# Spreading x in f32, and joining the norm stage to the scan

## The chip, the cores and the metric

One core of a Trainium2 chip runs one program. Its five engines have a queue each: TensorE (PE, with its weight loads shown as PEld), VectorE (DVE), ScalarE (ACT), GpSimd (POOL) and SyncE (SP), which issues the DMAs. The metric is the device time of one execution in microseconds.

## The reference, cut to what matters

```python
x = sequence                                  # (1, 4096, 256)
x = x + ssm(layernorm(x))                     # the part that is changed
x = x + ffn(layernorm(x))
x = x + attention(layernorm(x))               # 16 heads of 16, 4096 x 4096 scores
x = x + ffn(layernorm(x))

def ssm(s):                                   # D = 256 channels, N = 16 states
    Bm, Cm = s @ W_B.T + b_B, s @ W_C.T + b_C
    Delta = softplus(s @ W_Delta.T + b_Delta + bias_Delta)     # one per position
    A_bar = exp(A * Delta)                                     # per channel and state
    B_bar = 1 / A * (A_bar - 1) * Bm
    state[t] = state[t-1] * A_bar[t] + s[t] * B_bar[t]
    y[t] = sum over the 16 states of state[t] * Cm[t]
```

All of it is f32. The four sums over positions and heads of the attention are the bulk of the kernel's time and are not touched by the change.

## The kernel before, in words

**Norm stage** (`norm_and_project`, up to line 412). The 4096 positions are taken in 8 chunks of 512. For a chunk, DVE takes statistics and normalises (L224, L228, L240), PE transposes the chunk (`turn`, L393), ACT copies the transposed f32 chunk out of PSUM (`copy_turned`, L330), and PE projects it (`project` in the new code, L408) to B, C and Delta, which are replicated so that each of the 128 partitions holds the value of its state; ACT adds the biases (`outputs`, L344). For the scan, the f32 values are also split into three bf16 parts, whose sum is the f32 value: ACT rounds (L334), POOL subtracts (L212), ACT rounds the rest (L338), DVE subtracts again (L247). DVE and ACT compute softplus by quarters of 1024 positions: -|z| (`minus_abs`, L254), exp (L350), log (L354), and the sum (L259). The FFN weights' angles are prepared beside this (L278 to L289). The stage is a block of its own: all engines meet at its end before the next block's first instruction.

**Scan stage** (`scan_to_projection`). A tile is 8 channels x 16 states on 128 partitions, by 1024 positions; 32 tiles cover the channels and 4 quarters the positions, so 128 tiles, n = 0 to 127, in that order. For a tile:
- PE spreads 8 channels of x over 128 partitions (`spread_x`, L717): a product with a 0/1 matrix, 2 halves of 512 positions, each the sum of three bf16 products. Its result goes to the PSUM pair `xr`, in the first tiles also to `yb`; `xr` is single, so the spread of tile m waits until DVE has read that of tile m-1 (`w_done`).
- DVE multiplies it by B (`times_b`, L969) into one of six buffers `w`.
- ACT computes the decay exp(A Delta) into PSUM (L871), and for the tiles of POOL a second time into SBUF, minus one (`decay_less_one`, L857, L860). Its carry out of a tile is saved by ACT (L864).
- Five of eight tiles have `w` multiplied by decay minus one on POOL (`u`, L1113), three (n mod 8 = 0, 3, 6) on DVE (`own_u`, L980): `by_pool` says which.
- DVE scans (L999).
- POOL multiplies the states by C (L1122, `hc`, two buffers), and PE sums over the 16 states with the `gather` matrix (L749, f32, 2 halves, each with two records in the trace) into `yb`. After 16 tiles ACT copies `yb` out (`copy_y`), PE transposes it back (`turn_y`, L728) in the third tile of the next 16, through `xr`, and DVE adds it to x (`add_y`, L964).

The order is written out by hand. On DVE tile n is: the scan of n; `add_y` if n mod 16 = 3; then `times_b` of the tiles m with `scan_before(m) == n` (mostly m = n+4, in the first row later ones too) and `own_u(n+1)` if that is DVE's. On PE tile n is: the spreads m with `spread_after(m) == n` (mostly m = n+5; the spreads 7 and 8 of each 16 tiles come in one slot), then the gather of n. On POOL it is `hc` of n, then `u(n+3)`. On ACT: the decay of n, the carry of n-2, `copy_y`, and `decay_less_one(n+3)`; in a few early tiles there are also the late half of softplus and the sine of the FFN angles, each with a change of the activation table.

After the scan come the FFN units (L540, L553), the q, k, v projections (L760 to L805) and the attention.

Of the kernel before, what the change touches and what calls it, by code (L numbers as in the profile page):

```python
# [30 lines left out]
P = 128  # L31
# [100 lines left out]
def norm_and_project(nc, mem, io):  # L132

    with ExitStack() as ctx:
        def sb(name, shape, dt):
            return ctx.enter_context(nc.sbuf_tensor(name, shape, dt))

        w_bcd = place(mem, 136, [DH, 3, P])
        bias = sb("bias_bcd", [P, 4], F32)
        recip_a = sb("recip_a", [P, NJ], F32)  # L140
        mask = sb("channel_mask", [P, CPT], F32)
        xn = place(mem, 112, [2, TPC, D])
        xnt = place(mem, 120, [2, DH, CH])
        rest = place(mem, 128, [2, DH, CH])
        std = sb("np_std", [P, NT, 1], F32)
        noise = place(mem, 140, [DH, 2, D])
        turns = place(mem, 144, [DH, 2, D])
        ang = mem.w_ffn[:].rearrange("p h (a o) -> p h a o", a=2)
        tp = ctx.enter_context(nc.psum_tensor("np_tp", [P, DH, CH], F32))
        pb = ctx.enter_context(nc.psum_tensor("np_proj", [P, 2, 3, CH], F32))  # L150
        (loaded, consts, pool_step, gather_step, sums_done, stats_done, std_ready, rstd_ready, xn_ready, t_ready, xnt_ready,
         hi_ready, rest_ready, mid_ready, lo_ready, proj_ready, proj_read, neg_ready, exp_ready, ln_ready, bias_ready,
         soft_added, angles_loaded, angle_step, table_step) = make_sems(
            nc, ctx, "np", "loaded consts poolstep gatherstep sums stats std rstd xn t xnt hi rest mid lo proj projread neg "
            "exp ln bias softadded anglesloaded anglestep tablestep")
        x_loaded = make_sems(nc, ctx, "np", " ".join(f"x{i}" for i in range(NC)))

        def tiles(i):
            return slice(i * TPC, (i + 1) * TPC)

        def cols(i):
            return slice(i * CH, (i + 1) * CH)

        def quarter(q):
            return slice(q * SC, (q + 1) * SC)

        with nc.Block() as block:
            @block.sync
            def _(sp):
                xv = io.x.rearrange("a (t p) d -> (a p) t d", p=P)  # L170
                for i in range(NC):
                    sp.dma_start(mem.x[:, tiles(i), :], xv[:, tiles(i), :]).then_inc(x_loaded[i], 16)
                    if i == 0:
                        sp.dma_start(w_bcd, io.w_bcd.rearrange("(h p) j c -> p h j c", p=P)).then_inc(loaded, 16)
                        sp.dma_start(bias[:], io.bias_bcd).then_inc(loaded, 16)
                        sp.dma_start(mem.a_scale[:], io.a_tiles).then_inc(loaded, 16)
                for n, (w, e) in enumerate(((io.theta, io.theta_noise), (io.phi, io.phi_noise))):
                    sp.dma_start(ang[:, :, n, :], w.rearrange("(h p) o -> p h o", p=P)).then_inc(angles_loaded, 16)
                    sp.dma_start(noise[:, :, n, :], e.rearrange("(h p) o -> p h o", p=P)).then_inc(angles_loaded, 16)

            @block.gpsimd
            def _(pool):
                steps = Chain(pool, pool_step)

                steps.link(nc.gpsimd.memset(mem.eps[:], EPS))
                steps.link(nc.gpsimd.memset(mem.ident[:], 0.0))
                steps.link(nc.gpsimd.affine_select(
                    out=mem.ident[:], in_=mem.ident[:], compare_op=ALU.not_equal, fill=1.0, base=0,
                    pattern=[[-1, P]], channel_multiplier=1))
                pool.sem_inc(consts, 1)  # L190

                steps.link(nc.gpsimd.memset(mask[:], 1.0))
                steps.link(nc.gpsimd.affine_select(out=mask[:], in_=mask[:], compare_op=ALU.is_ge, fill=0.0, base=0,
                                                   pattern=[[-NS, CPT]], channel_multiplier=1))
                steps.link(nc.gpsimd.affine_select(out=mask[:], in_=mask[:], compare_op=ALU.is_ge, fill=0.0,
                                                   base=NS - 1, pattern=[[NS, CPT]], channel_multiplier=-1))
                steps.link(nc.gpsimd.memset(mem.gather, 0.0))
                pool.sem_inc(consts, 1)
                steps.link(nc.gpsimd.tensor_copy(mem.ident_b[:], mem.ident[:]))
                steps.link(nc.gpsimd.memset(mem.spread, 0.0))  # L200
                v = mem.spread.rearrange("p j (a n) -> p j a n", n=NS)
                steps.link(nc.gpsimd.affine_select(
                    out=v, in_=v, compare_op=ALU.not_equal, fill=1.0, base=0,
                    pattern=[[-CPT, NJH], [-1, CPT], [0, NS]], channel_multiplier=1))
                steps.link(nc.gpsimd.memset(mem.carry[:], 0.0))

                def what_hi_leaves(i):

                    pool.wait_ge(hi_ready, i + 1)
                    if i >= 2:  # L210
                        pool.wait_ge(lo_ready, i - 1)
                    nc.gpsimd.tensor_tensor(rest[:, i % 2], xnt[:, i % 2], mem.xp[:, 0, :, cols(i)],  # L212
                                            ALU.subtract).then_inc(rest_ready, 1)

                for i in range(NC):
                    what_hi_leaves(i)

            @block.vector
            def _(dve):
                def stats(i):  # L220

                    dve.wait_ge(x_loaded[i], 16)
                    for t in range(i * TPC, (i + 1) * TPC):
                        last = nc.vector.bn_stats(mem.six[:, t, :], mem.x[:, t, :])  # L224
                    last.then_inc(sums_done, 1)
                    dve.wait_ge(sums_done, i + 1)
                    for t in range(i * TPC, (i + 1) * TPC):
                        last = nc.vector.bn_aggr(mem.mv[:, t, :], mem.six[:, t, :])  # L228
                    last.then_inc(stats_done, 1)

                def normalise(i):

                    dve.wait_ge(std_ready, i + 1)
                    nc.vector.reciprocal(mem.rstd[:, tiles(i), :], std[:, tiles(i), :]).then_inc(rstd_ready, 1)
                    dve.wait_ge(rstd_ready, i + 1)
                    if i >= 2:
                        dve.wait_ge(t_ready, i - 1)
# [351 lines left out]
def scan_before(m):  # L589

    if m < 4:
        return 0
# [1243 lines left out]
```

## Time and profile before

| | us |
|---|---|
| median of 3 runs | 3477.95 (3476.05 to 3478.55) |
| the profiled execution | 3478.46 |
| its span, first to last instruction | 3476.6 |
| norm stage, to the first spread of the scan stage | 0 to 77.6 |
| first scan to the start of the last scan | 83.51 to 593.16 |
| the rest (FFN, projections, attention, FFN) | to 3476.6 |

In the whole span PE is busy 96%, DVE 94%, ACT 78%, POOL 24%. Those are averages over stages that are limited by different engines; the rows of the stages that the change touches are in the section below. Of a row, the first number is the start in us from the span's start, the second the time from the start to the end of the last instruction of the row; "[0.43 <-PE banks L717]" means that the engine was idle 0.43 us before it and that a PE instruction of line 717 released it. Matmuls follow each other faster than the duration of one: an instruction's result is there only some time after the next has started.

### The profile page before, as it was taken

How to read it: one execution, taken by the hardware profiler on the slowest of the kernel's cores; microseconds unless marked ns; L12 is line 12 of the kernel's file. 1: busy time of each engine (PE TensorE's matmuls, PEld its weight loads, DVE VectorE, ACT ScalarE, POOL GpSimd, SP SyncE). 2: the span in 40 equal slices, each digit the busy share in tenths (PEclk: the TensorE clock that was granted, in tenths of full speed). 3: DMA queues.
4: the chain of work that ended last, by engine and by line, in shares of the span. 5: the costliest groups of instructions: out<-in, count | busy, mean ns of one | idle time of the engine just before them, and what ended most of it. 6: DMA issues, size and time to landing. Idle time of an engine off the chain costs nothing.

```text
span 3476.6 us, 59741 instructions
## 1 busy us (share of the span) xinstructions
PE 3330.3 (96%) x22826; PEld 1192.6 (34%) x22852; DVE 3260.1 (94%) x4960; ACT 2718.5 (78%) x4991; POOL 830.4 (24%) x707
## 2 busy tenths in 40 slices
PE   6788888989999999999999999999999999999999
PEld 3222222542333333333333333333333333333334
DVE  7899999589999999999999999999999999999943
ACT  6766665756888888888888888888888888888865
POOL 3899998662000000000000000000000000000004
PEclk9999999988999999999999999999999999999999
DMA  2000001052020120202020202112020202020011
GB/s 65 1 10 0 1 1 49 31 149 30 6 33 13 28 30 10 33 6 33 8 33 6 33 6 33 25 16 33 6 33 6 36 6 33 6 33 6 8 55 49
DMA packets 53678, 87.11 MB, mean 25 GB/s; under 512 B 13200, under 2 KB 40464, under 8 KB 49232
## 3 DMA queue, kind: packets, MB, share of 16 engines
q1 hardware_dynamic: 53200, 82.77, 12.6%
q8 instruction: 179, 2.93, 0.4%
q14 instruction: 107, 0.88, 0.1%
q10 hardware_dynamic: 192, 0.52, 0.1%
HBM read 53.37 MB, written 21.23 MB: 21 GB/s over the span
## 4 chain that ended last, share of the span: by engine, by line
PE 81%; DVE 10%; issue 4%; POOL 1%; ACT 1%; DMA 0%; DVEq 0%; SPq 0%; POOLq 0%; ACTq 0%
PE banks L1493 29%; PE banks L1450 16%; PE banks L1445 15%; PE banks L1408 11%; DVE arena L999 5%; PE banks L553 3%; DVE arena L969 3%; PE banks L1406 2%; PE banks L805 1%; DVE arena L1666 1%; DVE arena L980 1%; PE banks L797 1%; PE banks L1515 1%; POOL arena L1122 0%; POOL arena L1113 0%
## 5 line engine op out<-in xcount | busy, mean ns | idle before, releaser
L1649 DVE TENSOR_REDUCE arena<-banks 128x1 f32<-128x512 f32 x4032 | 2503.7, 683 | 19.1 <-PE banks L1408 15.5
L1623 ACT ACTIVATE arena<-banks 128x512 f32<-128x512 f32 x4096 | 2114.9, 602 | 417.0 <-PE banks L1445 409.5
L1445 PE MATMUL banks<-arena 64*128 64x512 bf16 x4032 | 1245.8, 379 | 0.0
L1450 PE MATMUL banks<-arena 35*128 35x512 bf16 x4032 | 1207.2, 378 | 0.6 <-DMA arena<-max_rows 0.4
L1493 PE MATMUL banks<-arena 128*32 128x512 f32 x8192 | 1090.8, 605 | 0.0
L1406 PE MATMUL banks<-arena 64*128 64x512 bf16 x2048 | 789.2, 387 | 22.9 <-DVE arena L1666 20.2
L1408 PE MATMUL banks<-arena 64*128 64x512 bf16 x2048 | 786.9, 386 | 0.6 <-DVE arena L1649 0.6
L1445 PEld LDWEIGHTS banks<-arena 64*128 64x128 bf16 x4032 | 375.8, 93 | 391.7 <-PE banks L1450 5.7
L1408 PEld LDWEIGHTS banks<-arena 64*128 64x128 bf16 x2048 | 188.2, 93 | 796.6 <-DVE arena L1649 792.4
L1450 PEld LDWEIGHTS banks<-arena 35*128 35x128 bf16 x4032 | 358.0, 93 | 157.7 <-ACT arena L1623 8.7
L1373 POOL TENSOR_TENSOR arena<-arena 64x512 f32<-64x512 f32 x64 | 81.2, 1268 | 1191.6 <-DMA arena<-arena 1157.2
L1122 POOL TENSOR_TENSOR arena<-arena 128x1024 f32<-128x1024 f32 x128 | 301.7, 2369 | 30.3 <-DVE arena L999 30.0
L1341 POOL CAST neg_parts<-neg_max 128x8 bf16<-128x8 f32 x64 | 12.2, 191 | 1239.3 <-DVE neg_max L1661 1239.3
L999 DVE TENSOR_TENSOR_SCAN arena<-banks,carry,arena 128x1024 f32<-128x1024 f32 x128 | 299.2, 2338 | 1.0 <-POOL arena L1122 1.0
L749 PE MATMUL banks<-arena 128*32 128x512 f32 x512 | 247.7, 607 | 41.2 <-POOL arena L1122 41.2
L871 ACT ACTIVATE banks<-arena,a_scale 128x1024 f32<-128x1024 f32 x128 | 142.8, 1116 | 142.3 <-DVE arena L999 141.6
L1493 PEld LDWEIGHTS banks<-arena 128*32 128x32 f32 x8192 | 161.2, 108 | 237.9 <-issue 230.8
L717 PE MATMUL banks<-arena 128*128 128x512 bf16 x742 | 189.6, 389 | 51.7 <-DVE arena L969 39.2
L1406 PEld LDWEIGHTS banks<-arena 64*128 64x128 bf16 x2048 | 190.9, 94 | 52.8 <-DVE arena L1666 26.8
L1113 POOL TENSOR_TENSOR arena<-arena 128x1024 f32<-128x1024 f32 x79 | 189.0, 2393 | 15.3 <-DVE arena L969 15.3
L969 DVE TENSOR_TENSOR arena<-banks,arena 128x1024 f32<-128x1024 f32 x128 | 154.0, 1204 | 11.9 <-PE banks L717 11.9
L717 PEld LDWEIGHTS banks<-arena 128*128 128x128 bf16 x768 | 65.9, 99 | 219.0 <-DVE arena L969 121.6
(137 smaller groups left out, 1730.7 us busy)
## 6 DMA issues: line engine op xcount, KB each, us to landing
arena<-qk_parts SPq DMA_DIRECT2D x242, 128.0 KB, 7.1
qk_parts<-arena SPq DMA_DIRECT2D x32, 384.0 KB, 2.6
arena<-arena SPq DMA_DIRECT2D x63, 128.0 KB, 2.3
x_res<-in_x SPq DMA_DIRECT2D x8, 512.0 KB, 7.9
arena<-in_trig SPq DMA_DIRECT2D x2, 2048.0 KB, 9.0
arena<-qk_parts SPq DMA_DIRECT2D x64, 64.0 KB, 10.9
att_t<-arena SPq DMA_DIRECT2D x128, 32.0 KB
arena<-att_t SPq DMA_DIRECT2D x8, 512.0 KB, 5.5
```

Of the source, the lines that this page charges most:

```text
L717: last = nc.tensor.matmul(x_bank(n)[:, b * CH:(b + 1) * CH], mem.spread[:, j % NJH, :], mem.xp[:, part, j // NJH, c * SC + b * CH:c * SC + ...
L749: last = nc.tensor.matmul(yb[32 * g:32 * g + 32, b * CH:(b + 1) * CH], mem.gather[:, j, :], hc[:, n % 2, b * CH:(b + 1) * CH], start=(r == ...
L969: nc.vector.tensor_tensor(w[:, n % WBUF, :], x_bank(n), mem.b_rep[:, cols(n)], ALU.mult).then_inc(w_done, 1)
L999: nc.vector.tensor_tensor_scan(st[:, n % 2, :], decay[:, n % 2, :], w[:, n % WBUF, :], mem.carry[:, j:j + 1], ALU.mult, ALU.add).then_inc( ...
L1122: nc.gpsimd.tensor_tensor(hc[:, n % 2, :], st[:, n % 2, :], mem.c_rep[:, cols(n)], ALU.mult).then_inc(hc_done, 1)
L1406: return nc.tensor.matmul(out, q_twin[LANE:P, par, q], k_twin[LANE:P, par, c // 2, :], start=True, stop=True)
L1408: return nc.tensor.matmul(out, q_rows[0:LANE, par, q], k_rows[0:LANE, par, c * CH:(c + 1) * CH], start=True, stop=True)
L1445: return nc.tensor.matmul(sc[:, (4 * t + j) % SB, :], k, q, start=(j == 1), stop=(j != 1))
L1450: return nc.tensor.matmul(sc[:, (4 * t + j) % SB, :], k, q, start=(j != 1), stop=(j == 1))
L1493: last = nc.tensor.matmul(acc[32 * j:32 * j + VW, :], v_ones[:, h % 2, 2 * kp + j // 2, :], prob[:, t % PBUF, j * CH:(j + 1) * CH], start= ...
L1623: nc.scalar.activation(prob[:, t % PBUF, j * CH:(j + 1) * CH], sc[:, n % SB, :], ACT.Exp, scale=SCALE).then_inc(exp_done, 1)
L1649: nc.vector.tensor_reduce(part_max[:, b % 2, u // NC, u % NC:u % NC + 1], mx[:, unit_bank(b, u), :], AXX, ALU.max).then_inc(dve_read, 1)
```

## The change

It has these parts:
- **x in f32.** The transposed chunk is copied once, in f32, into `x_t`; the three bf16 parts and the instructions that make them are gone (L334, L338 of ACT, L212 of POOL, L247 of DVE). A spread is one f32 product for each half, instead of three bf16 products; the 0/1 matrix is f32 too. The projections read `x_t` as well.
- **No barrier.** The norm stage's five queues are put ahead of the scan stage's in one block; the PSUM banks are shared, and waits on the norm stage's semaphores take the barrier's place (`proj_read`, `soft_added`, `consts`, `gather_step`, `angle_step`, `neg_ready`). PE's queue goes: spread 0, projection of the last chunk, spread 1, a wait for all projections to be read, spreads 2 and 3. The outputs of the last chunk come behind the first decay on ACT, and the last quarter's `minus_abs` behind tile 3 on DVE.
- **The first products.** `times_b(1)` moves behind the first scan; in the first tiles two products follow each scan. `own_u(1)` is DVE's now, not POOL's.
- Late exps and the sine of the angles come one tile later on ACT.

```diff
 def by_pool(n):
-    return n % 8 not in BY_DVE and n < NT_SCAN - 1
+    return n % 8 not in BY_DVE and 1 < n < NT_SCAN - 1

 def scan_before(m):
-    if m < 4:
-        return 0
-    if m < 6:
-        return 1
+    if m < 7:
+        return (m - 1) // 2
     return m - 3 if m > NJH and m % NJH in (7, 8) else m - 4
...
-        return yb if n in (1, 3) else xr
+        return yb if n in (0, 1, 3) else xr
...
         def spread_x(n):
-            if n > 1:
-                pe.wait_ge(w_done, n if n > 3 else n - 1)
+            if n > 0:
+                pe.wait_ge(w_done, n if n > 3 else max(1, n - 1))
...
-                for part in range(NPART):
-                    last = nc.tensor.matmul(
-                        x_bank(n)[:, b * CH:(b + 1) * CH], mem.spread[:, j % NJH, :],
-                        mem.xp[:, part, j // NJH, c * SC + b * CH:c * SC + (b + 1) * CH],
-                        start=(part == 0), stop=(part == NPART - 1))
+                last = nc.tensor.matmul(
+                    x_bank(n)[:, b * CH:(b + 1) * CH], mem.spread[:, j % NJH, :],
+                    mem.x_t[:, j // NJH, c * SC + b * CH:c * SC + (b + 1) * CH], start=True, stop=True)
...
-        for n in range(4):
-            spread_x(n)
+        pe.wait_ge(mem.norm.consts, 3)
+        spread_x(0)
+        mem.norm.project(pe, NC - 1)
+        spread_x(1)
+        pe.wait_ge(mem.norm.proj_read, NC)
+        spread_x(2)
+        spread_x(3)
+        pe.wait_ge(mem.norm.gather_step, 5)
...
         for n in range(NT_SCAN):                      # ACT
             if n >= 2:
                 act.wait_ge(scan_done, n - 1)
+            if n < 2:
+                act.wait_ge(mem.norm.proj_read, NC - 1 + n)
             soft_here(n)
...
-            if n == 5:
+            if n == 0:
+                mem.norm.outputs(act, NC - 1)
+            if n == 6:
                 late_exps()
...
-            if n == 7:
-
+            if n == 8:
+                act.wait_ge(mem.norm.angle_step, 10)
                 nc.scalar.activation(mem.w_ffn[:], mem.w_ffn[:], ACT.Sin)
...
         times_b(0)                                    # DVE
         own_u(0)
-        times_b(1)
...
-            ahead = [m for m in range(2, NT_SCAN) if scan_before(m) == n]
+            ahead = [m for m in range(1, NT_SCAN) if scan_before(m) == n]
             own = n + 1 < NT_SCAN and not by_pool(n + 1)
-            if own and len(ahead) == 2:
+            if own and len(ahead) >= 2:
                 times_b(ahead.pop(0))
...
+            if n == 3:
+                mem.norm.minus_abs(dve, NSC - 1)
...
             def copy_turned(i):                       # ACT, norm stage
                 act.wait_ge(t_ready, i + 1)
-                    if i >= 2:
-                        act.wait_ge(proj_ready, i - 1)
-                        act.wait_ge(rest_ready, i - 1)
-                    nc.scalar.activation(xnt[:, i % 2], tp[:], ACT.Copy).then_inc(xnt_ready, 1)
+            nc.scalar.activation(mem.x_t[:, :, cols(i)], tp, ACT.Copy).then_inc(xnt_ready, 1)
...
-                    high(i)
-                    if i >= 1:
-                        middle(i - 1)
-                        outputs(i - 1)
+            if i >= 1:
+                outputs(act, i - 1)
...
-                for i in range(NC):
-                    what_hi_leaves(i)
...
-                    if i >= 1:
-                        low(i - 1)
...
-        mem.xp = place(mem, 0, [NPART, DH, S], BF16)
+        mem.x_t = place(mem, 0, [DH, S])
-        mem.spread = place(mem, 160, [NJH, P], BF16)
+        mem.spread = place(mem, 32, [NJH, P])
...
-                for part in (middle, last):
+                for part in (first, middle, last):
```

## Rows read from the trace of the kernel before

**Rows 1.** Windows: busy us and instructions by engine, granted clock, DMA share, GB/s.
```profile
300.00:400.00 100.00, 85.45 (x264) 23.22 (x267) 99.13 (x63) 67.04 (x84) 96.09 (x43) 1.00 0.00 1
```

**Rows 2.** Groups by line, 0 to 700 us: busy, mean ns, idle before.
```profile
L1122 POOL TENSOR_TENSOR arena<-arena 128x1024 f32<-128x1024 f32 x128 | 301.7, 2369 | 30.3 <-DVE arena L999 30.0
L999 DVE TENSOR_TENSOR_SCAN arena<-banks,carry,arena 128x1024 f32<-128x1024 f32 x128 | 299.2, 2338 | 1.0 <-POOL arena L1122 1.0
...
L969 DVE TENSOR_TENSOR arena<-banks,arena 128x1024 f32<-128x1024 f32 x128 | 154.0, 1204 | 11.9 <-PE banks L717 11.9
```

**Rows 3.** Timeline of DVE in tiles 53 and 54.
```profile
302.57 2.33 DVE L999 TENSOR_TENSOR_SCAN arena<-banks,carry,arena 128x1024 f32<-128x1024 f32 x1
304.82 1.20 DVE L969 TENSOR_TENSOR arena<-banks,arena 128x1024 f32<-128x1024 f32 x1
305.94 1.21 DVE L980 SCALAR_TENSOR_TENSOR arena<-banks,arena 128x1024 f32<-128x1024 f32 x1
307.58 1.23 DVE L969 TENSOR_TENSOR arena<-banks,arena 128x1024 f32<-128x1024 f32 x1 [0.43 <-PE banks L717]
```

**Rows 4.** Timeline of PE: gather, spread, gather in the scan.
```profile
260.42 1.90 PE L749 MATMUL banks<-arena 128*32 128x512 f32 x4 [1.24 <-POOL arena L1122]
262.25 1.47 PE L717 MATMUL banks<-arena 128*128 128x512 bf16 x6
263.65 1.90 PE L749 MATMUL banks<-arena 128*32 128x512 f32 x4
```

**Rows 5.** Timeline of PE behind the scan: a gather, then f32 products with 128x128 weights.
```profile
602.24 1.90 PE L749 MATMUL banks<-arena 128*32 128x512 f32 x4
604.07 1.98 PE L553 MATMUL banks<-w_ffn,arena 128*128 128x512 f32 x4
605.89 0.60 PE L540 MATMUL banks<-ident,arena 128*128 128x128 f32 x4
```

**Rows 6.** Timeline of POOL in the scan.
```profile
279.11 2.36 POOL L1122 TENSOR_TENSOR arena<-arena 128x1024 f32<-128x1024 f32 x1 [0.20 <-DVE arena L999]
```

**Rows 7.** Groups of weight loads, by form.
```profile
L717 PEld LDWEIGHTS banks<-arena 128*128 128x128 bf16 x768 | 65.9, 99 | 219.0 <-DVE arena L969 121.6 <-issue 38.9
...
L553 PEld LDWEIGHTS banks<-w_ffn,arena 128*128 128x128 f32 x128 | 22.8, 190 | 22.9 <-issue 22.9
```

**Rows 8.** Timeline of PE, norm stage and the first spread.
```profile
48.45 5.32 PE L408 MATMUL np_proj<-arena 128*128 128x512 f32 x12
54.93 1.07 PE L393 MATMUL np_tp<-ident,arena 128*128 128x128 f32 x8 [1.16 <-issue]
...
77.61 2.76 PE L717 MATMUL banks<-arena 128*128 128x512 bf16 x6 [9.35 <-PEq L167]
```

**Rows 9.** Timeline of ACT at the end of the norm stage.
```profile
60.89 1.84 ACT L344 ACTIVATE arena<-np_proj,bias_bcd 128x512 f32<-128x512 f32 x3
...
64.04 2.00 ACT L354 ACTIVATE arena<-arena 128x1024 f32<-128x1024 f32 x2
```

**Rows 10.** Timeline of DVE, one removed subtraction of the norm stage.
```profile
61.02 2.30 DVE L247 TENSOR_TENSOR arena<-arena 128x1024 bf16<-128x1024 f32 x1 [3.92 <-ACT arena L338]
```

**Rows 11.** Timeline of PE in the first tiles.
```profile
88.16 2.70 PE L717 MATMUL banks<-arena 128*128 128x512 bf16 x6 [3.04 <-DVE arena L969]
91.85 3.49 PE L749 MATMUL banks<-arena 128*32 128x512 f32 x4 [0.99 <-POOL arena L1122]
95.26 1.47 PE L717 MATMUL banks<-arena 128*128 128x512 bf16 x6
```

**Rows 12.** Timeline of DVE: the scans 2 and 5, `own_u(8)`.
```profile
97.91 2.34 DVE L999 TENSOR_TENSOR_SCAN arena<-banks,carry,arena 128x1024 f32<-128x1024 f32 x1
...
109.16 2.34 DVE L999 TENSOR_TENSOR_SCAN arena<-banks,carry,arena 128x1024 f32<-128x1024 f32 x1
...
120.06 1.23 DVE L980 SCALAR_TENSOR_TENSOR arena<-banks,arena 128x1024 f32<-128x1024 f32 x1 [0.68 <-ACT banks L871]
```

**Rows 13.** Timeline of DVE: the last wait of a scan.
```profile
584.16 2.35 DVE L999 TENSOR_TENSOR_SCAN arena<-banks,carry,arena 128x1024 f32<-128x1024 f32 x1 [0.97 <-POOL arena L1122]
```

More of the change, by code:

```diff
@@ L837, in late_exps @@
             for q in range(LATE, NSC):
+                act.wait_ge(mem.norm.neg_ready, q + 1)
                 nc.scalar.activation(mem.soft[:, q, :], mem.soft[:, q, :], ACT.Exp).then_inc(exp_ready, 1)
@@ L845, in soft_here @@
         def soft_here(n):
+            if n // NJ < LATE and n % NJ < 4:
+                act.wait_ge(mem.norm.soft_added, n // NJ + 1)
             if n // NJ >= LATE and n % NJ < 4:
@@ L968, in times_b @@
             dve.wait_ge(xr_ready, n + 1)
+            if n % NJ == 0:
+                dve.wait_ge(mem.norm.proj_read, 2 * (n // NJ) + 2)
             nc.vector.tensor_tensor(w[:, n % WBUF, :], x_bank(n), mem.b_rep[:, cols(n)], ALU.mult).then_inc(w_done, 1)
@@ L992, in scan_tile @@
                 dve.wait_ge(u_dve, n - pool_before(n) + 1)
+            if n == 0:
+                dve.wait_ge(mem.norm.consts, 3)
             if n >= 2:
@@ L1119, in gpsimd @@
             pool.wait_ge(scan_done, n + 1)
+            if n % NJ == 0:
+                pool.wait_ge(mem.norm.proj_read, 2 * (n // NJ) + 2)
             if n >= 2:
@@ L1765, in hybrid_kernel @@
         mem.sums = nc.dram_tensor("att_sums", [2, H * QC, CH], F32, kind="Internal").ap()
-        norm_and_project(nc, mem, io)
         mem.banks = ctx.enter_context(nc.psum_tensor("banks", [P, 8, CH], F32))
+        first = norm_and_project(nc, mem, io, ctx)
         middle, last = scan_to_projection(nc, mem, io, ctx), attention(nc, mem, io, out, ctx)
@@ L1776, in _ @@
             def _(pe):
-                for part in (middle, last):
+                for part in (first, middle, last):
                     part[1](pe)
@@ L1781, in _ @@
             def _(act):
-                for part in (middle, last):
+                for part in (first, middle, last):
                     part[2](act)
@@ L1786, in _ @@
             def _(dve):
-                for part in (middle, last):
+                for part in (first, middle, last):
                     part[3](dve)
@@ L1791, in _ @@
             def _(pool):
-                for part in (middle, last):
+                for part in (first, middle, last):
                     part[4](pool)
```

432 lines of the change are left out of this document (206 added, 226 removed).

## The prediction, made before the changed kernel ran

> **What bounds the kernel now.** I read the windows first. In 300 to 400 us, inside the scan stage, DVE is busy 99.13 of 100 us, POOL 96.09 and PE 85.45 [rows 1]. DVE sets the pace, but POOL and PE are close behind. The groups name the work of a tile: a scan of 2.34 us, a product of 1.20 on DVE, an `hc` of 2.37 on POOL, and 11.9 us in which `times_b` waited for a spread, nearly all in the first tiles [rows 2]. The timelines then give the pitch, start to start, which counts rather than the duration. On DVE the scan takes 2.26 (302.57 to 304.82), `times_b` and `own_u` 1.12 each (304.82 to 305.94) [rows 3]. Eight tiles with three `own_u` are thus 8 x 3.38 + 3 x 1.12 = 30.4 us; sixteen, with one `add_y` of about 1.12 and the one wait of 0.43, are 62.4. That wait is the only place of the period in which a spread is late now: `times_b(57)` behind `own_u(54)` [rows 3].
>
> **The f32 spread, in the steady scan.** PE's pitch: a gather 1.83 (260.42 to 262.25), a bf16 spread 1.40 (262.25 to 263.65), with its result 1.47 after its start [rows 4]. The trace of before has no f32 spread; the nearest rows are four f32 records with the same shapes (128x128 weights, 512 columns) right behind a gather: pitch 1.82 (604.07 to 605.89), result after 1.98; a gather, with 32 columns of weights, has 1.90 [rows 5]. I take 1.82 and 1.98. So PE has 16 x (1.83 + 1.82) + about 1.0 for `turn_y` = 59.4 us of work in 62.4 us. It fits on average, but the spread buffer `xr` is single. A spread may start only 0.13 after the `times_b` before it ended, while the next one wants it 2.26 later, or 3.38 with an `own_u` between. With PE free, 0.13 + 1.98 + 0.03 = 2.14 is just in time. Where PE is still in a gather, it isn't.
>
> I walked PE, DVE and POOL (2.31 an operation, a gather 0.11 behind its `hc` [rows 6], which must not start before the scan's end) through tiles 40 to 64 in queue order, by hand. Two kinds of places came out late:
> - Once in 16 tiles, where spreads 56 and 57 have two scans less to hide in: from the end of `times_b(55)`, spread 56 starts at 0.13, gather 51 (ready) follows for 1.83, spread 57 starts at 0.13 + 1.82 + 1.83 = 3.78, its result is usable at 3.78 + 2.01 = 5.79. DVE comes for it at 2.26 + 1.12 + 1.12 = 4.50. It waits 1.29 instead of 0.43: +0.86. The next one, through gather 52, is late 0.27 more (4 PE steps against 1.12 + 2.26). With the rest of that half row: +1.19.
> - In each other eight tiles, two or three waits of about 0.15, where PE starts a spread 0.27 late behind a gather that waited for POOL: +0.32.
>
> There are 7 rows of the first kind (k = 1 to 7) and 8 half rows of the second: 7 x 1.19 + 8 x 0.32 = 10.9 us longer. Bounds: with the 0.15s gone (PE 0.1 faster at each step) 7 x 0.86 = 6.0, and if the result came as early as a gather's (0.08 less), 5.5; with the weight loads exposed 24 (rival B). I take 10.9, as the stand-in rows have the same shapes. The tile work of DVE, POOL and ACT has no other change.
>
> A weight load of a bf16 spread is 99 ns, of f32 at the same shape 190 [rows 7]. In the f32 group above, the four loads lie inside a pitch of 1.82 [rows 5]. The Trainium skill, "TensorE: Matmul & The Clock Gate", section "Weight-path perf modes — Fast Weight Load (FWL) and DoubleRow", says that weights are loaded fast only when there are 128 of them and they are not FP32. The trace agrees with its ratio of about two. By that page the change gives the fast load away in every spread; by the row it costs nothing beyond the pitch above.
>
> **The front.** PE sets the norm stage's pace: a projection 5.15 (5.32 less the overlap), a transposition 0.87. PE ran without a gap to 53.6, where transposition 7 (54.93) was 1.16 late, since DVE had not normalised; and the first spread came at 77.61, after 9.35 idle [rows 8]. What lay between was the tail of ACT (outputs 60.89, logs 64.04 [rows 9]) and DVE: a removed subtraction is 2.30 and waited 3.92 for ACT [rows 10]. In the new order, each time from the end of what it waits for:
> - Transposition 7 at 53.6 (DVE has 8 subtractions less; it is ready near 45), projection 6 at 54.5, spread 0 at 59.6, projection 7 from 61.4 to 66.6.
> - ACT: outputs 5 at 55.6, table load and logs to 60.7, outputs 6 to 62.5, a table load of 1.3 and the first decay to 65.0. DVE: both softplus sums to 62.1, `times_b(0)` to 63.3, `own_u(0)` 65.1, first scan 66.2. Before it was 83.5: 17.3 earlier.
> - ACT's outputs 7 at 66.8, decay 1 to 69.7; DVE `times_b(1)` 68.6, `own_u(1)` 69.8, `times_b(2)` 70.9, second scan 72.1. ACT has made `less` of tile 2 by 71.9; POOL `u(2)` from 72.2, `hc(0)` to 76.8. `times_b(3)` at 74.4 frees `yb`.
> - Gather 0 at 76.9, and spread 4 stands behind it. PE has then been idle since spread 3 ended at 72.4, for 4.5 us. In the trace of before, a gap of 3.04 was followed by a spread of 2.70 instead of 1.47 and a gather of 3.49 instead of 1.90, the 1.2 GHz level; at 95.26 it was back at 2.4 [rows 11]. I take gather 0 at 3.4, spread 4 at 2.0: `times_b(4)` at 82.3, scan 2 at 83.4. It was 97.91 [rows 12]: 14.5 earlier.
> - Then part of it is given back. Products 5 and 6 now both stand behind scan 2: one product more there, 1.1, and `times_b(6)` waits about 1.3 for its spread, since PE has gather 1 between spreads 5 and 6. `minus_abs(3)`, which lay in the norm stage's tail, now costs DVE 1.1 behind tile 3. Scan 5 starts at 98.3, was 109.16 [rows 12]: 10.9 earlier.
>
> Bounds: 12.5 if the clock does not fall (gather 0 1.6 shorter), 7.5 if spreads 4 and 5 run at 1.2 GHz as well. I take 10.9. The spread matrix in f32 is twice the memset and select of POOL, under the loading of x, and is wanted only at 59.6: nothing. SP's DMAs keep their order, no transfer is added. `late_exps` and the sine one tile later: the sine's 0.68 wait of `own_u(8)` [rows 12] falls away, since in the slot of tile 8 ACT has no `less` to make (tile 11 is DVE's): -0.7. The logs' stall stays. At the scan's end DVE waited 0.97 for POOL [rows 13]; a slower DVE finds POOL less far behind: -0.3.
>
> **Sum.** -10.9 - 0.7 - 0.3 + 10.9 = -1.0 us, against the profiled execution's own 3478.46 (0.5 above the median of the runs): 3477.5. Nothing behind the scan changes.
>
> **Rivals.**
> - A, PE keeps its cover: the 0.15 and 0.27 waits don't exist, because PE, POOL and DVE settle into a phase where gathers fall between the spreads, and the clock holds in the front. -12.5 - 0.7 - 0.3 + 6.0 = -7.5: 3471. For it: PE has 3 us free in 62.4, DVE has shown a single wait in a period, and each DVE wait lets POOL get ahead. Against it: the 1.29 hangs on nothing that can settle.
> - B, PE becomes the bound, slower than before: the f32 weight loads of a spread aren't hidden. If the first two (0.30 for a pair) stand before the products, a spread is 2.01 and PE's sixteen tiles take 16 x 3.84 + 1.0 = 62.4, as long as DVE's: this is the point from which PE decides. The `times_b(57)` wait grows by two spreads' excess to 1.67, the next by 0.38, and the small ones double: about 3.2 in 16 tiles, 24 in the stage: 3478.5 - 11.9 + 24 = 3490.5. For it: 190 against 99 ns. Against it: the 1.82 of [rows 5].
> - C, the barrier's time isn't there to take: the five queues start the scan behind the same work, because ACT (logs, outputs 6, outputs 7, two table loads) is the longest chain, and the scan gains 5 instead of 10.9: 3483. Against it: ACT loses 16 roundings (about 1 us each).
>
> **How the numbers follow.** This kernel's runs tell 0.2% (7 us) from no change. Forecast 0.5, A 0.25, B 0.15, C 0.1. The forecast's own range, from its bounds (front 7.5 to 12.5, scan 6 to 14), is 3471 to 3484. The 8-in-10 range reaches to A's and most of the way to B's: 3467 to 3487. Faster by over 0.2%: nearly half of A's and a part of the forecast's case that meets the better ends of both, 0.27. Slower: B and a little of C, 0.18. Within: 0.55.
>
> **What would show it.** Changed profile: the first scan near 66 and scan 5 near 98 (front right or wrong); the f32 spread's start-to-start with the gather behind it 1.82, its record group 1.98; DVE waiting for a spread about 1.3 once in 16 tiles at the tile with n mod 16 = 9, and idle some 10 us in the whole scan; DVE's busy share in 300 to 400 near 97, PE's near 97; scan start of tile 127 minus that of tile 5 about 10 longer than 484.0. Wrong would be: DVE waits of half a microsecond at most tiles (B), or none but the large one (A), or a granted clock under 1.0 in the middle of the scan.

## The result, and the profile after

The changed kernel takes 3484.61 us (median of 16 runs, 3482.49 to 3486.25), the kernel before 3477.80 (16 runs, 3475.70 to 3480.62): ratio 1.0019, interval 1.0013 to 1.0026. That is 6.8 us slower, where 1 us faster was forecast. The profiled execution took 3483.62, its span 3481.7: 5.2 more than before's. The other 1.6 us lie between the profiled executions and the medians (before's is 0.7 above its median, after's 1.0 below).

The window of 300 to 400 us, which answers to [rows 1]:

```profile
300.00:400.00 100.00, 96.60 (x211) 26.86 (x210) 95.84 (x61) 64.14 (x81) 92.83 (x41) 1.00 0.00 0
```

PE is now the busiest (96.60, was 85.45); DVE has fallen to 95.84 and POOL to 92.83. The clock is 1.00 as before. The groups of the page, answering to [rows 2] and [rows 7]:

```profile
L980 DVE TENSOR_TENSOR_SCAN arena<-banks,carry,arena 128x1024 f32<-128x1024 f32 x128 | 299.5, 2340 | 0.4 <-POOL arena L1107 0.3
...
L949 DVE TENSOR_TENSOR arena<-banks,arena 128x1024 f32<-128x1024 f32 x128 | 155.0, 1211 | 25.1 <-PE banks L683 25.1
L683 PEld LDWEIGHTS banks<-arena 128*128 128x128 f32 x512 | 87.0, 189 | 198.5 <-DVE arena L949 119.8
```

Durations on DVE have not moved (2338 and 2340 ns, 1204 and 1211), so the loss is in waits: `times_b` (L949) waits 25.1 us for the spread, it was 11.9. Where in the scan, the timeline of DVE says (it answers to [rows 3]):

```profile
302.07 1.21 DVE L960 SCALAR_TENSOR_TENSOR arena<-banks,arena 128x1024 f32<-128x1024 f32 x1
304.60 1.23 DVE L949 TENSOR_TENSOR arena<-banks,arena 128x1024 f32<-128x1024 f32 x1 [1.32 <-PE banks L683]
305.74 2.34 DVE L980 TENSOR_TENSOR_SCAN arena<-banks,carry,arena 128x1024 f32<-128x1024 f32 x1
308.35 1.23 DVE L949 TENSOR_TENSOR arena<-banks,arena 128x1024 f32<-128x1024 f32 x1 [0.27 <-PE banks L683]
...
317.37 2.34 DVE L980 TENSOR_TENSOR_SCAN arena<-banks,carry,arena 128x1024 f32<-128x1024 f32 x1
319.90 1.23 DVE L949 TENSOR_TENSOR arena<-banks,arena 128x1024 f32<-128x1024 f32 x1 [0.20 <-PE banks L683]
321.04 2.34 DVE L980 TENSOR_TENSOR_SCAN arena<-banks,carry,arena 128x1024 f32<-128x1024 f32 x1
```

In 16 tiles there is one wait of 1.32, one of 0.27 and three of 0.20. Start to start each costs more than its bracket says: 304.60 - 302.07 is 2.53 where 1.12 was the pitch, so 1.41; 319.90 - 317.37 is 2.53 against 2.26, so 0.27 for a bracket of 0.20, and with the next step (1.14 for 1.12) 0.30. DVE operations that follow each other at once overlap by some 0.08, and a wait loses that too. Sixteen tiles take 64.58 (tile 64 to tile 80), before 62.41: +2.18, which is 0.90 + 0.38 + 3 x 0.30.

PE beside it (answers to [rows 4] and [rows 5]), then its weight loads at the first of these spreads and gathers:

```profile
302.58 1.98 PE L683 MATMUL banks<-arena 128*128 128x512 f32 x4
304.50 1.90 PE L720 MATMUL banks<-arena 128*32 128x512 f32 x4
306.33 1.98 PE L683 MATMUL banks<-arena 128*128 128x512 f32 x4
```
```profile
302.58 0.30 PEld L683 LDWEIGHTS banks<-arena 128*128 128x128 f32 x2 [0.84 <-DVE arena L949]
...
304.49 0.14 PEld L720 LDWEIGHTS banks<-arena 128*32 128x32 f32 x2 [0.76 <-issue]
```

A spread has a pitch of 1.92 (302.58 to 304.50), not the 1.82 of the forecast; a gather keeps 1.83. The first weights of a spread load from 302.58, when the gather before is done, not under it. Sixteen spreads and gathers are 60.0 us, with the turn's transpositions about 61, in 64.58.

The front, on DVE (answers to [rows 12]) and PE (answers to [rows 8] and [rows 11]):

```profile
66.06 2.35 DVE L980 TENSOR_TENSOR_SCAN arena<-banks,carry,arena 128x1024 f32<-128x1024 f32 x1
...
71.85 2.34 DVE L980 TENSOR_TENSOR_SCAN arena<-banks,carry,arena 128x1024 f32<-128x1024 f32 x1
...
82.34 1.23 DVE L949 TENSOR_TENSOR arena<-banks,arena 128x1024 f32<-128x1024 f32 x1 [7.04 <-PE banks L683]
83.48 2.34 DVE L980 TENSOR_TENSOR_SCAN arena<-banks,carry,arena 128x1024 f32<-128x1024 f32 x1
...
93.91 2.48 DVE L172 SCALAR_TENSOR_TENSOR arena<-arena 128x1024 f32<-128x1024 f32 x1
96.31 2.34 DVE L980 TENSOR_TENSOR_SCAN arena<-banks,carry,arena 128x1024 f32<-128x1024 f32 x1
...
99.69 2.33 DVE L980 TENSOR_TENSOR_SCAN arena<-banks,carry,arena 128x1024 f32<-128x1024 f32 x1
...
124.50 1.22 DVE L960 SCALAR_TENSOR_TENSOR arena<-banks,arena 128x1024 f32<-128x1024 f32 x1 [3.04 <-ACT banks L847]
...
129.48 1.22 DVE L949 TENSOR_TENSOR arena<-banks,arena 128x1024 f32<-128x1024 f32 x1 [0.37 <-PE banks L683]
...
134.33 1.23 DVE L949 TENSOR_TENSOR arena<-banks,arena 128x1024 f32<-128x1024 f32 x1 [1.37 <-PE banks L683]
```
```profile
76.86 3.46 PE L720 MATMUL banks<-arena 128*32 128x512 f32 x4 [4.78 <-POOL arena L1107]
80.26 2.05 PE L683 MATMUL banks<-arena 128*128 128x512 f32 x4
...
126.91 2.53 PE L683 MATMUL banks<-arena 128*128 128x512 f32 x4 [2.96 <-DVE arena L949]
129.37 3.00 PE L720 MATMUL banks<-arena 128*32 128x512 f32 x4
```

The best single view of the two traces is the start of each tile's scan, after less before, in us. The last row is a kernel of the experiments, the change's f32 spread with the barrier kept:

| tile | 0 | 2 | 5 | 8 | 10 | 13 | 15 | 64 | 112 | 124 | 127 |
|---|---|---|---|---|---|---|---|---|---|---|---|
| changed | -17.45 | -14.43 | -9.47 | -10.26 | -9.97 | -8.22 | -8.23 | -2.00 | +4.52 | +6.40 | +5.75 |
| barrier kept | -6.58 | -7.66 | -7.35 | -7.62 | -7.32 | -8.06 | -8.07 | -1.18 | +5.33 | +7.20 | +6.56 |

The scan starts 17.45 us earlier and gives back 8.0 of them in the first five tiles and 1.2 up to tile 15; from there to tile 124 it loses 14.6 more, 2.18 in a full period of 16 tiles. Between tile 127's scan and the end the changed kernel is 0.65 quicker.

Each trace is one execution, and executions differ before any edit can act. The four kernels with the f32 spread and no barrier are alike up to the first scan, yet it starts at 66.06, 66.44, 65.51 and 67.64. In three of the bf16 kernels without the barrier it starts at 78.45, 77.38 and 76.04. A difference of 1 or 2 us at tile 0 between two such kernels is therefore not the edit's.

### The profile page after: what moved, and what is told of

Its sections match the earlier page's. It is cut to its first block, busy times and chain, and to the rows that moved or that the text cites. A ratio compares the mean times of both kernels' runs of the same rounds, so it can differ in the third digit from the quotient of the medians.

```text
span 3481.7 us, 59214 instructions
## 1 busy us (share of the span) xinstructions
PE 3389.3 (97%) x22596; PEld 1211.3 (35%) x22596; DVE 3244.9 (93%) x4953; ACT 2699.4 (78%) x4973; POOL 810.5 (23%) x698
## 4 chain that ended last, share of the span: by engine, by line
PE 85%; DVE 9%; issue 3%; ACT 2%; POOL 1%; DMA 0%; SPq 0%; DVEq 0%; POOLq 0%; ACTq 0%
PE banks L1478 29%; PE banks L1435 16%; PE banks L1430 15%; PE banks L1393 11%; DVE arena L980 5%; PE banks L522 3%; DVE arena L949 2%; PE banks L1391 2%; PE banks L683 2%; PE banks L776 1%; PE banks L720 1%; DVE arena L1651 1%; ACT banks L847 1%; PE banks L187 1%; PE banks L768 1%
## 5 line engine op out<-in xcount | busy, mean ns | idle before, releaser
L980 DVE TENSOR_TENSOR_SCAN arena<-banks,carry,arena 128x1024 f32<-128x1024 f32 x128 | 299.5, 2340 | 0.4 <-POOL arena L1107 0.3
L683 PE MATMUL banks<-arena 128*128 128x512 f32 x512 | 253.8, 619 | 27.5 <-DVE arena L949 26.0
L949 DVE TENSOR_TENSOR arena<-banks,arena 128x1024 f32<-128x1024 f32 x128 | 155.0, 1211 | 25.1 <-PE banks L683 25.1
L683 PEld LDWEIGHTS banks<-arena 128*128 128x128 f32 x512 | 87.0, 189 | 198.5 <-DVE arena L949 119.8
```

Of the source, the lines that this page charges most:

```text
L683: last = nc.tensor.matmul(x_bank(n)[:, b * CH:(b + 1) * CH], mem.spread[:, j % NJH, :], mem.x_t[:, j // NJH, c * SC + b * CH:c * SC + (b + ...
L949: nc.vector.tensor_tensor(w[:, n % WBUF, :], x_bank(n), mem.b_rep[:, cols(n)], ALU.mult).then_inc(w_done, 1)
L980: nc.vector.tensor_tensor_scan(st[:, n % 2, :], decay[:, n % 2, :], w[:, n % WBUF, :], mem.carry[:, j:j + 1], ALU.mult, ALU.add).then_inc( ...
```

## The experiments

Theory P is the prediction's with the measured pitch: the single spread buffer and PE's queue make a few spreads late. L says that only the latency of an f32 spread counts, N that the joining brings nothing. Each median stands against the kernel before on the same chip.

**The f32 spread alone, barrier kept.**

```diff
-                for part in range(NPART):
-                    last = nc.tensor.matmul(..., mem.xp[:, part, j // NJH, ...],
-                        start=(part == 0), stop=(part == NPART - 1))
+                last = nc.tensor.matmul(..., mem.x_t[:, j // NJH, ...], start=True, stop=True)
```

> The kernel before with the f32 spread alone: one f32 copy, no bf16 splits, the barrier and the order of the first tiles kept. Theory P (PE's work per tile decides: a spread 1.92 and a gather 1.83, start to start, with one spread buffer): 16 tiles take 64.6 us instead of 62.4, as in the changed kernel, the places where DVE waits are the same (1.3 once, 0.27 once, 0.2 three times), 15 us in the stage. The norm stage without its splits ends 9 us earlier (the last projection 3 us earlier, and no subtraction, two roundings behind it). Sum 3478 + 15 - 9 = 3484, so the missing barrier itself is worth nearly nothing. Theory J (the loss comes from joining the stages: other placements, other clock): 16 tiles stay at 62.4, 3469.

Measured: 3484.05 us (11 runs, 3479.51 to 3491.43), ratio 1.0018, interval 1.0009 to 1.0027. The profiled execution is the slowest of the 11; its last scan starts 6.56 us behind before's, and 6.5 us more lie behind the scan stage, so it is compared up to the last scan only. Sixteen tiles take 64.57. Two waits of DVE:

```profile
305.42 1.23 DVE L938 TENSOR_TENSOR arena<-banks,arena 128x1024 f32<-128x1024 f32 x1 [1.32 <-PE banks L687]
...
309.17 1.23 DVE L938 TENSOR_TENSOR arena<-banks,arena 128x1024 f32<-128x1024 f32 x1 [0.27 <-PE banks L687]
```

The same waits, and the same median as the whole change within 0.6 us. The scan's slope belongs to the f32 spread alone. And the table shows more: the barrier kept, the first scan comes 10.9 us later than in the changed kernel, and at tile 15 it is 0.16 apart. All that the joining gains is spent in fifteen tiles. The 8 us that both kernels still have there come with the f32 form, whose norm stage has no roundings.

**Latency or PE's queue: half of each gather.**

```diff
-            for b in range(SC // CH):
+            for b in range(1):
```

> The changed kernel with only the first half of each gather (the sum over the states is left out for the second 512 positions of each tile). Theory P: PE has 0.86 us less per tile, the 0.2 and 0.27 waits of DVE vanish, the large one falls from 1.32 to about 1.0 (what is left is the f32 spread's own 1.98 behind times_b(56)); 16 tiles take 63.0, 3473. Theory L (the waits come from the latency of the f32 spread behind the product before it, whatever PE does else): the waits stay, 16 tiles 64.6, 3484.

Measured: 3474.27 us (10 runs), ratio 0.9989 (0.9980 to 0.9998). Sixteen tiles take 62.92, and the only wait in them is this:

```profile
298.58 1.21 DVE L960 SCALAR_TENSOR_TENSOR arena<-banks,arena 128x1024 f32<-128x1024 f32 x1
300.74 1.23 DVE L949 TENSOR_TENSOR arena<-banks,arena 128x1024 f32<-128x1024 f32 x1 [0.95 <-PE banks L683]
```

With PE relieved of 0.9 us in each gather the 0.20s and the 0.27 are gone and 0.95 of 1.32 stays. So 0.51 us in 16 tiles over before is what a slower spread costs by itself: the wait is 0.52 longer than before's 0.43, and a spread's result takes 0.51 longer (1.98 against 1.47). The other 1.66 of the 2.18 need the whole gathers in its way. L falls, P holds. (Each tile's sum lacks half its positions here, so the kernel's result is not the reference's.)

**The barrier's removal alone: the bf16 parts back.** The changed kernel with `high`, `middle`, `low` and `what_hi_leaves` again, and the spread of before:

```diff
+            if j == 0:
+                pe.wait_ge(mem.norm.lo_ready, 2 * c + 2)
...
+                for part in range(NPART):
+                    last = nc.tensor.matmul(..., mem.xp[:, part, j // NJH, ...],
+                        start=(part == 0), stop=(part == 2))
```

> The changed kernel with the three bf16 parts back: the splits made in the norm stage as in the kernel before (the middle and low part of the last chunk behind tile 1), no barrier, the new order of the first tiles. Theory P (PE's work per tile decides): 16 tiles at 62.4 us again, one DVE wait of 0.4 in them; the first scan later than the changed kernel's 66.1, at about 73, since ACT's queue has its roundings back, scan 2 near 88; 3468 to 3471. Since the f32 spread with the barrier kept took 3484.05 as well, the joined stages were worth nothing there; if that holds with bf16 too (theory N: what joining gains in the front is always given back in the first 16 tiles), this one is at 3478.

Measured: 3479.57 us (11 runs), ratio 1.0004 (0.9995 to 1.0013). The interval holds a ratio of 1, so no gain or loss is shown. Sixteen tiles take 62.41, with one wait of 0.43, as before. The first scan was missed by 5 us:

```profile
68.56 2.50 DVE L316 TENSOR_SCALAR w_ffn<-w_ffn 128x1024 f32<-128x1024 f32 x1
...
78.45 2.35 DVE L1021 TENSOR_TENSOR_SCAN arena<-banks,carry,arena 128x1024 f32<-128x1024 f32 x1
```

The range reduction of the angles and the roundings (62.11 to 73.38) stand on DVE ahead of the softplus sums, as they did before; I had left them out. The scans' differences are -5.06 at tile 0, +1.31 at tile 5, +2.66 from tile 13. So 6.4 us are given back by tile 5, as 8.0 are in the f32 kernel; 2.4 of them in either kernel come between scans 3 and 4, where `minus_abs(3)` stands, and the rest with the new order of the products. The logs' stall costs another 1.3. For the front N was right.

**Array time or weight loads: four bf16 products.** The kernel just shown, the second part added twice, so that a spread holds the array as long as in f32 but loads bf16 weights:

```diff
-                for part in range(NPART):
+                for part in (0, 1, 1, 2):
```

> As bf16_joined, but each half of a spread is four bf16 products instead of three (the second part is added twice, so x is off by its second part): the array work of an f32 product, with bf16 weight loads of 99 ns instead of f32 ones of 190. If the exposed f32 weight load counts: a spread is 1.83 start to start instead of 1.92, the small waits shrink, and 16 tiles take 63.9; 10 us over bf16_joined. If only the array work counts: 1.92, 64.6, 15 us over bf16_joined.

Measured: 3490.36 us (4 runs), ratio 1.0035 (1.0021 to 1.0048), 10.8 over the kernel just shown. Sixteen tiles take 63.85; the waits in them are 1.16 and 0.18 in place of 1.32 and 0.27, and none of 0.20 is left. PE:

```profile
286.83 1.90 PE L721 MATMUL banks<-arena 128*128 128x512 bf16 x8
288.66 1.90 PE L759 MATMUL banks<-arena 128*32 128x512 f32 x4
```

Its spread has a pitch of 1.83 where f32's has 1.92; the first load is 99 instead of 190 ns [rows 7], and 0.09 is that difference. Of the 2.17 us that f32 adds in 16 tiles, 1.44 come with the fourth pass over the array, and 0.73 with those 0.09 us in each spread. That the 0.09 is the weight load is read from the two equal differences; no run of a spread changes the load alone.

**The front's order.** In the changed kernel POOL made `u(2)` ahead of `hc(0)`, which gather 0 waits for, and `minus_abs(3)` stood on the path at 93.91. Here `hc(0)` comes first, and `minus_abs(3)` goes into the 7 us gap before `times_b(4)`:

```diff
-        for n in range(1, 3):
-            u(n)
+        u(1)
...
+            if n == 0:
+                u(2)
...
+                if m == 4:
+                    mem.norm.minus_abs(dve, NSC - 1)
-            if n == 3:
-                mem.norm.minus_abs(dve, NSC - 1)
```

> The changed kernel (f32) with two moves in the first tiles: POOL makes hc(0) before u(2), and the last quarter's minus_abs stands before times_b(4), where DVE waited 7.04 us, instead of behind tile 3, where it took 2.48. Theory P: times_b(4) comes when yb is free (times_b(3) done at 75.3), a gather 1.9 and a spread 2.0 later: 79.5 instead of 82.3, or 81 if PE still falls to 1.2 GHz in the gap; and scan 4 no longer has 2.5 in front: 4 to 5 us off, 3480. If the front isn't on the path (ACT or POOL late in tiles 5 to 16 anyway), under 1 us off.

Measured: 3480.31 us (10 runs), ratio 1.0009 (1.0000 to 1.0018), as expected. DVE at the gap, POOL beside it, and PE behind it:

```profile
74.66 2.60 DVE L172 SCALAR_TENSOR_TENSOR arena<-arena 128x1024 f32<-128x1024 f32 x1
81.47 1.22 DVE L949 TENSOR_TENSOR arena<-banks,arena 128x1024 f32<-128x1024 f32 x1 [4.21 <-PE banks L683]
```
```profile
73.83 2.36 POOL L1106 TENSOR_TENSOR arena<-arena 128x1024 f32<-128x1024 f32 x1
```
```profile
74.89 3.59 PE L720 MATMUL banks<-arena 128*32 128x512 f32 x4 [3.38 <-DVE arena L949]
78.42 3.02 PE L683 MATMUL banks<-arena 128*128 128x512 f32 x4
```

Scan 4 starts at -12.75, where the changed kernel had -9.48. Of these 3.3, 0.87 were there at scan 3, and of them 0.55 at the first scan already, which `hc(0)` has nothing to do with. Gather 0 began 2.0 earlier (74.89), but it took 3.59 and spread 4 3.02 (1.98 at full clock). So `hc(0)` first brings 0.3 to 0.9 in this execution. The other 2.4 are `minus_abs(3)`, which now costs nothing.

**The same two moves on the bf16 kernel.** Edit as above; `low(7)` stood in the gap already.

> bf16_joined with the same two moves. Theory P: the same 4 to 5 us off bf16_joined, 3464 to 3466, 12 under the kernel before. Theory N: 3478.

Measured: 3477.36 us (11 runs), ratio 0.9998 (0.9989 to 1.0007). This was missed by 12 us, with N's figure close: the scans' difference is -2.75 at tile 5 and -1.45 from tile 13. The expectation rested on a first scan near 73, as the one for the bf16 kernel above, on record at the same time; that scan came at 77.38. The moves themselves did what was expected of them: from +2.66 to -1.45 at tile 13 they take 4.1 off, 1.1 of which were there at the first scan. From -6.13 there to -1.45 the rest goes to the order of the products (3.4) and to the logs' stall (1.3 net).

**The logs off the path.** The late exponentials and logarithms of ACT stood at tiles 6 and 10, where the two table loads and 2.00 us of `logs` make `own_u(11)` late. At tile 3 ACT has time:

```diff
-            if n == 6:
-                late_exps()
-            if n == 10:
-                late_logs()
+            if n == 3:
+                late_exps()
+                late_logs()
```

> hc_first_gap (f32) with the late half's exps and logs on ACT at tile 3, where ACT waited 7.4 us for scan 2, instead of at tiles 6 and 10. If the logs' table loads are the cause of own_u(11)'s 3.04 wait, and the gap on PE behind it the cause of the 1.2 GHz products and of the waits of 0.37 and 1.37 behind that: all of it goes, 4.5 to 5 us, 3475.5 to 3476. If DVE would meet the next engine anyway: 2 us or less, 3478.5 and up. 16 tiles stay at 64.6 either way.

Measured for f32: 3477.81 us (11 runs), before 3477.14 there: ratio 0.9999 (0.9991 to 1.0008); the two medians alone give 1.0002. That is 1.8 us above the expected range and 2.5 under the kernel without the move, so about half of what was expected is there in the medians. The wait at `own_u(11)` is gone, and those of 0.37 and 1.37 behind it:

```profile
119.14 1.20 DVE L959 SCALAR_TENSOR_TENSOR arena<-banks,arena 128x1024 f32<-128x1024 f32 x1
```

Tile 13 starts at -15.13 (before the move -11.49); from tile 10 on, where the two stood at -12.19 and -12.94, the move brings 4.4. At tile 15 this execution is 3.6 ahead of the one without the move and at tile 127 3.0, since it waits 0.57 at tile 33 where the other has no wait. The scan's slope is 64.59 as ever.

> The same move in bf16_best. The stall at tile 11 and the one at tile 13 go: 3 to 4 us off its 3477.4, 3473.5 to 3474.5, with 16 tiles at 62.4; 4 under the kernel before. Otherwise 3476 and up.

Measured for bf16: 3471.16 us (11 runs, 3468.73 to 3473.86), ratio 0.9983 (0.9974 to 0.9992): 6 us less than the kernel before, with 1 outside the interval, and 13 less than the changed one. The lower end of the expected range is 2.3 us higher. Tile 13 starts at -8.90, and it is -8.87 at tile 127:

```profile
298.70 1.22 DVE L989 TENSOR_TENSOR arena<-banks,arena 128x1024 f32<-128x1024 f32 x1 [0.43 <-PE banks L721]
```
```profile
300.00:400.00 100.00, 87.22 (x270) 23.27 (x268) 99.57 (x63) 66.13 (x85) 95.81 (x43) 1.00 0.00 0
```

A gain of the front lasts to the end only where the scan's slope is before's. Of the 7.5 us that lie between this kernel and the one without the move (-1.45), 5.5 appear between tiles 10 and 13. The other 2.0 were there at tile 10 (-5.53 against -3.55), 1.3 of them at the first scan; they are not the logs'. The profiled execution is also the fastest of the 11: its scan stage ends 8.9 us ahead of before's, and the medians show 6.0. And no run moves the logs alone in the kernel with the barrier, so how much of the 6 us needs the joined stages is not shown.

## Why the prediction was wrong, step by step

The mechanism of the steady scan, a single spread buffer that a slower spread fills too late at a few places, is what the runs show. The steps that failed are three terms of the sum, all too favourable: the steady scan, priced from a pitch of 1.82 and from waits without their lost overlap; `minus_abs(3)` behind tile 3, priced at 1.1; and the logs' stall, taken as unchanged.

- **The sum.** Forecast -1.0; the scan's end came out at +5.75. The terms that were off: front to tile 5 -9.47 instead of -10.9 (+1.4); tiles 5 to 15 +1.25 instead of -0.7 (+1.95); the steady scan +14.6 instead of +10.9 (+3.7); the end -0.65 instead of -0.3 (-0.35); behind the scan -0.65 instead of 0. Together +6.1 on the profiled execution, whose difference is 5.2 and not -1.0. The three large ones had the same sign.
- **The steady scan: right in kind, mis-sized.** The large wait was forecast at 1.29 and is 1.32, at the tile named; the next 0.27 and is 0.27. The pair costs 1.28 in place of 1.13. The step that failed is the pitch of 1.82: the stand-in of [rows 5] was followed by a transposition, while before a gather it is 1.92. The trace of before could have told. The same four records with their first load under the product ahead have a pitch of 1.71 before a transposition (640.77 to 642.48) and of 1.82 before a gather (600.42 to 602.24 [rows 5]); the stand-in, whose first load is not hidden, has 1.82 before a transposition. Each of the two costs 0.1, and a spread pays both. That makes each small wait 0.20 instead of 0.15, and I priced them at the bracket, without the 0.08 of overlap that each one loses: 0.30 a piece, three in 16 tiles, against 0.32 + 0.06. This is +2.7 of the +3.7; the large pairs are the rest. The rows of before behind this:

```profile
600.42 1.88 PE L553 MATMUL banks<-w_ffn,arena 128*128 128x512 f32 x4
...
640.77 1.88 PE L553 MATMUL banks<-w_ffn,arena 128*128 128x512 f32 x4
...
642.48 0.60 PE L540 MATMUL banks<-ident,arena 128*128 128x128 f32 x4
```

- **The weight loads (rival B).** That the slow load "costs nothing beyond the pitch above" holds for 1.82: the 0.1 that is missing there goes with the gather behind the spread, as the rows just shown say. But the load is not free. By the same rows an f32 load that is not hidden lengthens the four records by 0.1, and by the four-product kernel 0.09 of the 1.92 go with f32 weights in place of bf16 ones. The rule of the Trainium skill weighed there ("TensorE: Matmul & The Clock Gate", section "Weight-path perf modes — Fast Weight Load (FWL) and DoubleRow") bears on 0.73 us in 16 tiles, some 5 us in the stage (an estimate, 7 x 0.73). B itself was too dear, 24 us where 14.6 came, since a spread is 0.09 longer than with four bf16 products, and not by the pair's 0.30. A (waits settle) is false: the pattern is the same in every period.
- **First tiles.** Right to 0.3 us: first scan 66.06 (66.2), second 71.85 (72.1), gather 0 at 76.86 with 3.46 (76.9 with 3.4), scan 2 at 83.48 (83.4), `times_b(6)` waiting 1.32 (1.3). Then `minus_abs(3)`: forecast 1.1 a step, measured 2.40. It has two SBUF inputs and stood beside an `hc` of POOL (the last section).
- **The sine** gave -0.79 at tile 8 (forecast -0.7). "The logs' stall stays" was too short: the wait of `own_u(11)` grew from 2.51 in the trace of before to 3.04, and behind it PE was idle for 2.96, so that the next spread took 2.53 and the gather 3.00, and DVE waited 0.37 and 1.37. This is not the f32 spread's doing: with bf16 parts and no barrier DVE waits 0.58 and 1.25 at the same places, and PE's two take 2.74 and 3.40 behind 3.49 of idle time. In the trace of before the first wait is 0.58 and the second does not exist; PE was idle for 3.42 there, and its two took 2.74 and only 2.10. With f32 and the barrier kept PE was idle for 2.55, lost nothing, and DVE waits only 0.20, at the second place. Why the joined kernels come out worse there is not shown.
- **What the joining is worth (rival C).** C put 3483 on "the barrier's time isn't there to take". The time was there: the first scan of the joined f32 kernel is 10.9 us ahead of that of the f32 kernel with the barrier. But at tile 5 the two stand at -9.47 and -7.35, and at tile 15 0.16 apart, so C was wrong in its reason and nearly right in what the joining leaves. The prediction never set the two halves of the change against each other: the f32 form alone makes the norm stage shorter, and the joining alone, in bf16, has a median 1.5 us above before's, with an interval that holds a ratio of 1. What pays is the order behind it: `minus_abs` in the gap and the logs early, and a little `hc(0)` first.
- **Chances.** Slower by over 0.2% had 0.18, and the measured 0.19% lies on the line. The direction was wrong; 3484.61 lies inside the 8-in-10 range and 0.6 above the forecast's own, whose upper bound of 14 for the scan is derived nowhere. The steady scan alone came to 14.6.

Still open: the 1.6 us between profiled executions and medians, which no run separates (behind the scan stage the profiled executions lie within 1.2 us of before's, but for the 6.5 of the f32 kernel with the barrier), and why an execution of the f32 kernels now and then skips or adds a wait (0.30 missing at tile 34 of the changed kernel, 0.66 there in two others).

## What to carry to other kernels

Before pricing a slower product on an engine that "fits on average", walk the single buffer between it and its reader, with the pitch read in front of the very instruction that will follow it, and price each wait start to start. A stage started earlier is worth what is left of it after the queues have filled: look for the first engine that idles there, and for what stands ahead of its releaser. Where a change has two halves, forecast each by itself.

## What the hardware showed that I had not expected

DVE operations with both inputs in SBUF do not run beside POOL here; they end 1.1 us after POOL's operation ends, and without POOL they take 1.2 in all. `minus_abs(3)` began at 93.91 and took 2.48, to 96.39, and POOL's `hc` ended at 95.30:

```profile
92.95 2.35 POOL L1107 TENSOR_TENSOR arena<-arena 128x1024 f32<-128x1024 f32 x1 [2.27 <-DVE arena L980]
```

In the kernel with `hc(0)` first it ended at 77.26, and POOL's operation at 76.19 (1.07). The removed subtraction of [rows 10] fits too: it ended at 63.32, POOL's last one at 62.24. The trace of before has four more like it, at 27.50, 33.52, 39.55 and 45.58, each 2.31 long and ending 1.08 or 1.09 after POOL's. Where POOL is idle, the same kinds of operation take 1.22:

```profile
71.15 1.22 DVE L254 SCALAR_TENSOR_TENSOR arena<-arena 128x1024 f32<-128x1024 f32 x1
```

`times_b` and `own_u`, with one input in PSUM, keep 1.20 beside POOL, and the scan its 2.34. The Trainium skill, "SBUF — State Buffer", section "Who interferes with whom", says of the port pair that the two engines share that "it's an exclusive lock", and that a DVE instruction with two SBUF inputs contends with a GpSimd instruction that reads SBUF. The traces agree, to 0.1 us; POOL came first in every case here. From these rows such an operation is priced at what is left of POOL's plus 1.1, not at its duration alone.

PE's clock in the front, as the granted clock (the column behind the five engines) of single operations: gather 0 and the spread behind it in the changed kernel, then the spread and the gather at tile 12:

```profile
76.86:80.26 3.40, 3.40 (x5) 0.47 (x5) 0.00 (x0) 1.30 (x3) 2.21 (x1) 0.52 0.00 0
80.30:82.30 2.00, 2.00 (x5) 0.70 (x4) 0.00 (x0) 0.00 (x0) 0.00 (x0) 0.97 0.00 0
...
126.91:129.40 2.49, 2.49 (x5) 0.71 (x6) 2.20 (x1) 1.12 (x2) 0.80 (x2) 0.76 0.00 0
129.40:132.30 2.90, 2.90 (x5) 0.51 (x4) 2.82 (x2) 0.99 (x2) 2.14 (x1) 0.62 0.00 0
```

Both times PE had been idle, for 4.78 and 2.96 us, and both times about 1.6 us were lost at the 1.2 GHz level before it was back at 2.4. Starting gather 0 2.0 earlier, after 3.38 of idle time, helped little in the kernel with `hc(0)` first: granted 0.50 in the gather and 0.65 in the spread, 2.7 us lost. With the logs early as well, PE did the same work ahead of it and was idle for 3.37, but the granted clock was 0.57 in the gather and 1.00 in the spread (3.23 and 1.98 us), 1.3 us lost. So the loss behind a gap differs by 1.4 us between two executions with the same gap, and one trace does not price it. An earlier start of work behind a gap may not be worth its whole lead.
